# A mixture-of-experts block: choices, ranks, contexts and weight pieces at other tiles, two early pairs, and a shift on ScalarE

## The reference

```python
xij = sigmoid(si[:, :, None] + sj[:, None, :] + b[0])     # si, sj: the context times two vectors
x = x + tanh(g_xattn) * (0.6 * xij + 0.4 * layernorm(x))
y = layernorm(x)                                          # tokens as rows
probs = softmax(y @ wg)                                   # 8 experts
idx, gate = argmax(probs), max(probs)
x = x + tanh(g_ffn) * gate * (y @ W[idx].T + b[idx])
```

## Time and profile before

| | us |
|---|---|
| median of three runs (610.95 to 768.54) | 611.22 |
| the profiled execution | 611.13 |
| its span, from first to last instruction | 609.5 |
| first product of the first expert starts | 177.3 |
| TensorE busy in the span | 521.3 |
| VectorE busy | 405.4 |
| POOL busy | 353.7 |
| ScalarE busy | 292.8 |

### The profile page before, as it was taken

One profiled execution on the slowest core, in us unless ns is written; L12 is line 12 of the kernel. 1 busy time (PEld: TensorE's weight loads), 2 busy tenths in 40 slices (PEclk: granted clock), 3 DMA queues, 4 the chain that ended last, 5 costly groups with the idle time before them and its releaser, 6 DMA issues.

```text
span 609.5 us, 14906 instructions
## 1 busy us (share of the span) xinstructions
PE 521.3 (86%) x2890; PEld 427.8 (70%) x2891; DVE 405.4 (67%) x538; ACT 292.8 (48%) x426; POOL 353.7 (58%) x536
## 2 busy tenths in 40 slices
PE   5577786566689993999999999999999999989980
PEld 5466675455568782888888888788888888878860
DVE  0866567899864675777777577877667757774330
ACT  2584656655522453554554445545354545453330
POOL 3685878875655551655645656556555565565651
PEclk9596778856759996999999999999999999999995
DMA  7942776997766675888888588798759867785520
GB/s 251 389 164 96 247 274 210 326 288 225 256 272 194 186 230 153 243 240 236 266 223 235 177 258 255 215 270 243 213 164 268 228 200 210 240 241 158 188 96 13
DMA packets 87755, 134.67 MB, mean 221 GB/s; under 512 B 11696, under 2 KB 69552, under 8 KB 87728
## 3 DMA queue, kind: packets, MB, share of 16 engines
q1 hardware_dynamic: 71504, 80.28, 46.9%
q0 software_dynamic: 15264, 54.06, 25.0%
q10 hardware_dynamic: 960, 0.00, 0.1%
HBM read 100.49 MB, written 35.91 MB: 224 GB/s over the span
## 4 chain that ended last, share of the span: by engine, by line
PE 34%; DVE 18%; issue 14%; POOL 10%; ACT 10%; ACTq 4%; POOLq 3%; DMA 3%; DVEq 1%; SPq 0%
PE pair L1241 24%; PE pair L1158 4%; DVE pair L929 3%; DVE xr L868 3%; DVE xt L921 3%; DVE raw L857 3%; ACT xt L714 3%; ACT rb L722 2%; POOL scal L559 2%; POOL scal L562 2%; DMA gates<-in_L_xattn_b 2%; PE pair L1149 2%; PE pair L1170 1%; ACT th L680 1%; DVE wt L908 1%
## 5 line engine op out<-in xcount | busy, mean ns | idle before, releaser
L1241 PE MATMUL pair<-wt,xt 128*128 (+1 forms) x1728 | 402.2, 395 | 13.0 <-DVE wt L937 12.9
L1241 PEld LDWEIGHTS pair<-wt,xt 128*128 128x128 f32 x1728 | 327.7, 190 | 87.1 <-issue 14.6
L921 DVE TENSOR_TENSOR xt<-pair,xt 128x1024 f32 (+1 forms) x38 | 46.5, 1225 | 68.3 <-ACT xt L714 68.3
L544 POOL TENSOR_TENSOR rows<-rows,rb 128x1024 f32<-128x1024 f32 x36 | 86.9, 2415 | 3.0 <-ACT rb L736 1.6
L708 ACT ACTIVATE wt<-pair 128x1024 f32 x54 | 55.5, 1028 | 58.0 <-DVE pair L929 54.2
L1158 PE MATMUL pair<-ident,xr 128*128 128x128 f32 x256 | 50.4, 362 | 36.9 <-DVE xr L868 36.9
L736 ACT ACTIVATE rb<-bias_bc,scal 128x1024 f32 (+1 forms) x37 | 46.0, 1244 | 70.6 <-POOL scal L566 70.6
L937 DVE TENSOR_TENSOR wt<-pair,wt 128x1024 f32 (+1 forms) x56 | 67.9, 1212 | 12.5 <-ACT wt L708 12.5
L1158 PEld LDWEIGHTS pair<-ident,xr 128*128 128x128 f32 x256 | 41.8, 192 | 44.1 <-DVE xr L868 36.1
L929 DVE STREAM_TRANSPOSE pair<-w_raw 128x1024 f32<-128x1024 f32 x56 | 69.4, 1240 | 3.5 <-DMA w_raw<-in_L_ffn_W 1.9
L579 POOL DMA_INDIRECT out_x<-rows,scatter_row x36 | 38.8, 1079 | 28.4 <-issue 26.9
(11 more groups left out here) (152 smaller groups left out, 420.0 us busy)
## 6 DMA issues: line engine op xcount, KB each, us to landing
w_raw<-in_L_ffn_W SPq DMA_DIRECT2D x264, 128.0 KB, 3.2
xb<-table SPq DMA_DIRECT2D x156, 128.0 KB
rows<-table POOLq DMA_DIRECT2D x38, 520.0 KB, 5.4
xr<-in_x SPq DMA_DIRECT2D x32, 512.0 KB, 7.3
ctx_in<-in_ctx SPq DMA_DIRECT2D x8, 512.0 KB, 6.1
bias_bc<-in_L_ffn_b SPq DMA_DIRECT2D x8, 512.0 KB, 6.7
out_x<-rows,scatter_row POOLq DMA_INDIRECT x36, 3.8
table<-xr,pos POOLq DMA_INDIRECT x32, 4.3
```

The costliest lines, as they stand in the source:

```text
L544: nc.gpsimd.tensor_tensor(rows[:, k, 0:H], rows[:, k, 0:H], rb[:, :], ALU.add).then_inc(base_ready, 1)
L921: nc.vector.tensor_tensor(xt[:, at, 1, :, :].rearrange("p a k n -> p (a k n)"), ps[:, :], xt[:, at, 0, :, :].rearrange("p a k n -> p (a k ...
L1241: last = nc.tensor.matmul(out_ps[r % 2][:, HALF * h:HALF * (h + 1)], xt[:, r % RING, x_part, k, :], wt[:, bass.ds(par, 1), w_part, k, HALF ...
```

## The change

The choice of a group g < 6 goes one tile later on VectorE, ahead of that tile's statistics; its rank goes ahead of the next tile's turns on TensorE, its position to that tile on VectorE; POOL's stores go one tile later each, and two more of group 6's stay at the last tile. The contexts 4 to 7 go to tiles 4, 7, 10 and 13, with ScalarE's steps one tile later each, ahead of the copy. The weight pieces go to earlier tiles, with the low part at the very next tile; SP's piece loads stand behind other tiles. ScalarE makes `ln_b` in a new function `shift`; POOL negates `ln_ma` once a group for it. Two pairs of the second expert are made before the slot loop.

```diff
-    WEIGHT_TILES = [18, 20, 21, 22, 24, 25, 26, 28]
-    ROW_TILES = [29, 31]
+    WEIGHT_TILES = [17, 18, 20, 21, 22, 24, 25, 26]
+    ROW_TILES = [28, 31]
+    EARLY_PAIRS = 2
+    PIECE_BEHIND = [27, 28, 30, 31]
...
-            return 2 * (g - 2) if g < 4 else GR * (g - 3)
+            return 2 * (g - 2) if g < 4 else 4 + 3 * (g - 4)
+        def chosen_at(g):
+            return GR * (g + 1) + (2 if g < NG - 2 else 1)
...
-                if t == RX + 8:
+                if t == RX + 7:
                     for m in range(WR):
                         load_piece(0, m)
-                if t in (RX + 11, RX + 14, RX + 15):
-                    m = {RX + 11: 3, RX + 14: 4, RX + 15: 5}[t]
+                if t in PIECE_BEHIND:
+                    m = WR + PIECE_BEHIND.index(t)
                     sp.wait_ge(w_turned, m - WR + 1)
                     load_piece(0, m)
...
+            for n in range(2):
+                sp.wait_ge(w_turned, K + n + 1)
+                load_next(K + 2 + n, n)
             for s in range(RX):
                 sp.wait_ge(row_stored[s], 16 * (T // RX))
...
                 link(nc.gpsimd.tensor_tensor(ln_ma[:, four], of_group(g, MEAN), ln_a[:, four], ALU.mult))
+                nc.gpsimd.tensor_scalar(ln_ma[:, four], ln_ma[:, four], -1.0, None, ALU.mult).then_inc(scales_of_tile, 1)
             def linear(t):
                 s = slot_of(t)
-                pool.wait_ge(th_ready, t + 1)
-                link(nc.gpsimd.tensor_scalar(ln_b[:, t:t + 1], xr[:, s, TH:TH + 1], nc2h[:, 0:1], ln_ma[:, t:t + 1],
-                                             ALU.mult, ALU.subtract))
+                pool.wait_ge(shift_ready, t + 1)
...
-                if r == 3 and g > 0:
-                    store(GR * (g - 1))
-                    store(GR * (g - 1) + 1)
-                if r < 2 and g > 1:
-                    store(GR * (g - 2) + 2 + r)
+                if r == 0 and g > 1:
+                    store(GR * (g - 2))
+                    store(GR * (g - 2) + 1)
+                if r in (1, 2) and g > 1:
+                    store(GR * (g - 2) + 1 + r)
...
+            def shift(t):
+                act.wait_ge(th_ready, t + 1)
+                act.wait_ge(scales_of_tile, t // GR + 1)
+                nc.scalar.activation(ln_b[:, t:t + 1], xr[:, slot_of(t), TH:TH + 1], ACT.Identity,
+                                     scale=nc2h[:, 0:1], bias=ln_ma[:, t:t + 1]).then_inc(shift_ready, 1)
...
                 if t + RTH - 1 < T:
                     half_tanh(t + RTH - 1)
+                for n in range(4, NG):
+                    if ctx_turn_tile(n) + 1 == t:
+                        context_copy(n)
+                    if ctx_turn_tile(n) + 2 == t:
+                        context_sums(n)
+                    if ctx_turn_tile(n) + 3 == t:
+                        context_spread(n)
                 if r == 1 and g > 0:
                     logits_copy(g - 1)
+                if t + RTH - 2 < T:
+                    shift(t + RTH - 2)
                 copy_turned(t)
...
-                if r == 2 and g > 0:
+                if g > 0 and chosen_at(g - 1) + 1 == t:
                     position(g - 1)
+                if g > 0 and chosen_at(g - 1) == t and g < NG - 1:
+                    choose(g - 1)
                 if t + LEAD < T:
                     stats(t + LEAD)
                     moments(t + LEAD)
-                if r == 1 and g > 0:
+                if r == 1 and g == NG - 1:
                     choose(g - 1)
...
-            link(nc.vector.tensor_scalar(kinds[:, :], n_begun[:, :], 1.0, None, ALU.is_equal))
+            link(nc.vector.tensor_scalar(kinds[:, :], n_begun[:, :], 1.0, float(EARLY_PAIRS), ALU.is_equal, ALU.mult))
...
+            dve.wait_ge(xt_ready, 2)
+            turn_pair(PAIRS, 0, cut_b)
+            turn_pair(PAIRS, 1, cut_a)
...
+            pair_low(PAIRS, 0, cut_b)
+            pair_low(PAIRS, 1, cut_a)
             finish(0, 0, 0, beyond_early[:, 0:1])
...
+                if g > 0 and chosen_at(g - 1) + 1 == t:
+                    rank(g - 1)
                 turn_tile(t)
...
-                if r == 2 and g > 0:
-                    rank(g - 1)
```

More of the change, by code:

```diff
@@ L225, in build @@
         lin_ready = sem("lin_ready")
+        scales_of_tile = sem("scales_of_tile")
+        shift_ready = sem("shift_ready")
         xc_ready = sem("xc_ready")
@@ L339, in _, with load_piece @@
             sp.dma_start(bias_bc[:, 0, :], bias[0:1, :].to_broadcast([P, H])).then_inc(bias_landed, 16)
+            def load_piece(e, m):
+                for q in (0, 2, 1, 3):
+                    sp.dma_start(w_raw[32 * q:32 * (q + 1), m % WR, :, :],
+                                 in_blocks(W[bass.ds(e, 1), P * m:P * (m + 1), :].rearrange("a o h -> (a o) h"),
+                                           q)).then_inc(w_landed[m % WR], 16)
             for g in range(4, 7):
@@ L344, in _ @@
             next_context(7)
-            def load_piece(e, m):
-                for q in (0, 2, 1, 3):
-                    sp.dma_start(w_raw[32 * q:32 * (q + 1), m % WR, :, :],
-                                 in_blocks(W[bass.ds(e, 1), P * m:P * (m + 1), :].rearrange("a o h -> (a o) h"),
-                                           q)).then_inc(w_landed[m % WR], 16)
             for t in range(RX + 2, T):
                 next_tile(t)
-                if t == RX + 8:
+                if t == RX + 7:
                     for m in range(WR):
                         load_piece(0, m)
-                if t in (RX + 11, RX + 14, RX + 15):
-                    m = {RX + 11: 3, RX + 14: 4, RX + 15: 5}[t]
+                if t in PIECE_BEHIND:
+                    m = WR + PIECE_BEHIND.index(t)
                     sp.wait_ge(w_turned, m - WR + 1)
                     load_piece(0, m)
-            for m in range(6, K):
-                sp.wait_ge(w_turned, m - WR + 1)
-                load_piece(0, m)
+            sp.wait_ge(w_turned, K - WR)
+            load_piece(0, K - 1)
             sp.wait_ge(th_ready, 3 * TB)
@@ L391, in _ @@
             for n in range(2):
-                sp.wait_ge(w_turned, K + n + 1)
-                load_next(K + 2 + n, n)
+                sp.wait_ge(w_turned, K + 2 + n + 1)
+                load_next(K + 4 + n, n)
             sp.wait_ge(xb_turned, 3)
@@ L533, in _ @@
                     linear(t + 2)
-                if r == 3 and g > 0:
-                    store(GR * (g - 1))
-                    store(GR * (g - 1) + 1)
-                if r < 2 and g > 1:
-                    store(GR * (g - 2) + 2 + r)
+                if r == 0 and g > 1:
[3 more added lines that the diff above has]
+                    store(GR * (g - 2) + 1 + r)
+                if t == T - 1:
+                    store(T - 2 * GR)
+                    store(T - 2 * GR + 1)
             for t in range(T - GR - 2, T):
@@ L748, in _ @@
                 context_spread(g)
+            act.wait_ge(scales_ready, 1)
             for t in range(RTH - 1):
                 half_tanh(t)
+                if t:
+                    shift(t - 1)
             for t in range(T):
@@ L763, in _ @@
                     xt_high(1, 1, cut_a)
-                for n in range(2, NG):
+                for n in range(2, 4):
                     if ctx_turn_tile(n) == t:
@@ L771, in _ @@
             logits_copy(NG - 1)
[L773 to L777, removed]
+            square(0, 0)
+            exp_sum(0, 0)
+            scaled_bias(0, 0, 0, 0)
             for n in range(RX):
@@ L781, in _ @@
                 cut_high(1, n, 1, ps)
+            square(1, 1)
+            exp_sum(1, 1)
+            scaled_bias(1, 1, 0, 0)
+            xt_high(2, 2, cut_a)
+            for n, ps in enumerate((cut_b, cut_a)):
+                cut_high(1, 2 + n, 1, ps)
             settled(summed, 2)
@@ L970, in _ @@
                 add_tanh(t)
+                if t - 1 in WEIGHT_TILES:
+                    cut_low(0, WEIGHT_TILES.index(t - 1), 0, cut_a)
                 if t in WEIGHT_TILES:
[L972 to L979, removed]
+                    dve.wait_ge(si_ready, NG)
+                    dve.wait_ge(sj_ready, NG)
+                    turn_weights(0, WEIGHT_TILES.index(t), cut_a)
+                if t == EARLY_TILES + GR + 1:
                     count_early()
                 if t == ROW_TILES[0]:
-                    cut_low(0, K - 1, 0, cut_a)
                     dve.wait_ge(w_ready, K)
@@ L1226, in _ @@
                         sum_context(n)
+                    if ctx_turn_tile(n) + (1 if n < 4 else 2) == t:
                         spread_context(n)
```

14 lines of the change are left out of this document (7 added, 7 removed).

## The result

Over 19 runs the changed kernel's median is 613.3 us against 610.1 for the kernel before; the ratio is 1.0051, with a 95% interval from 1.0031 to 1.0071. It is a little slower, and the forecast was 600.7. On that chip the medians were 617.8 and 610.38, ratio 1.0114 (1.0082 to 1.0146). The two intervals don't meet, and no run shows why the same kernel came out 4.5 us apart. The experiments are compared with 617.8, which like most of them is a median of four executions; measured from 613.3, what each of them brings back to the changed kernel is 4.5 less.

A forecast was written before the change was run, and what follows sets the result against it. VectorE was taken as the first stage's spine, with TensorE waiting for weights in the passage and full behind 240 us. From 611.13, minus 2.4 (first stage) and 8.0 (passage), came 600.7 us; range 590 to 614.

The forecast's parts named there:

- A7: End of VectorE's add of tile 7 in the first stage: forecast 54.3 us, 57.65 before.
- The logits and ranks together: VectorE's waits for logits by token and for ranks, first stage: together under 8 us; before, 16.9 and 9.2.
- Statistics wait for loads: First stage: new waits of VectorE's statistics on tile loads, 2 to 6 us in each of three groups.
- the row turn for its blocks: At tile 28, VectorE's row turn waits for the block loads, which need tile 19's store: 5.6 us.
- The chain behind A31: From tile 31's add (forecast 166.1) through turn, route, logits, choice, rank, totals to the first product (174.9): unchanged.
- passage: Passage to the second expert: second early pair shrinks TensorE's weight gap from 10.66 to 2.7; gain 8.0, between 5 and 10.7.
- three rounds of 17.8: Tiles 8 to 19, four per round: turn, copy, tanh, shift, scaling, store, load, statistics, add, 17.8 us each; 53.4 in all.
- A15: End of VectorE's add of tile 15 in the first stage: forecast 89.9 us, 95.34 before.
- A19: End of VectorE's add of tile 19 in the first stage: forecast 107.7 us, 6.5 earlier than before.
- A11: End of VectorE's add of tile 11 in the first stage: forecast 72.1 us, 76.23 before.
- The shift itself: ScalarE's shift per tile in the first stage, moved from POOL: taken as 0.25 us, between 0.17 and 0.4.
- Rival (b): Tiles 8 to 19: slower store and load landings make each round 24.6 us; total 621.1, slower than before; chance 0.12.

## Why the prediction was wrong

**Held.** A7 came at 54.75 for 54.3, with the mechanism named. The logits and ranks together wait 5.7, under the 8 forecast. Statistics wait for loads (11.1 in all, most of it in the first two rounds) and the row turn for its blocks (4.7, forecast 5.6). The chain behind A31 is unchanged: 186.91 - 178.2 = 8.7, before 8.8.

**The account**, by medians: passage 6.2, contexts 6.4 and pieces 2.3 won, 22.3 lost by late choices and ScalarE's shift, in all 7.4 slower (617.8 - 610.4). For the contexts the forecast had counted nothing.

**The step that failed: three rounds of 17.8.** They were 20.6, 18.0 and 23.8 (A15 is 93.3), 62.4 for 53.4, so A19 came 9.4 late and the first product 12.0 late. In the first round, 2.8 too long, the terms were: to the end of tile 10's scaling 8.0, where 6.5 and its handovers were summed (with the turn at 2.0, which took 1.1), store 5.4 for 4.1, load 4.3 for 4.0, statistics and add as summed. So the queues took 1.2 too much (2.1 with the turn as it was), the landings 1.6. The chain was the right one, its path through the queues and its landings mis-sized. The sum took each handover on ScalarE and POOL as a matter of 0.05, for which no row stood, that is, it followed one tile through the engines and let the queues stand empty. They weren't: ScalarE stood in front of an earlier shift, waiting for POOL, whose negation took 1.18 where 0.2 off the path was put down; and POOL's store stood behind a scaling, waiting for ScalarE. "ScalarE's order now decides when POOL may scale" stands in the prediction, as the reason to count no gain; that it is a loss was not priced. With the shift back on POOL, choices still late, the first round took 14.5 (A7 52.37, A11 66.82); the second and third took 20.6 and 21.1, with waits for loads and a weight piece.

The shift itself was a mis-sized term too: 0.39, not 0.25, at the top of its bounds. The row that it was taken from, a 128x4 activation of 0.17, has no scale or shift by column. The Trainium skill, "ScalarE: Activation LUTs", section "What ACT_TABLE_LOAD costs", gives 186 ns for a small activation and some 93 more for each operand that is a column; two of them make an estimated 0.37, and the trace agrees with 0.39. But this 0.14 a tile isn't the loss: the idle activations cost 1.1 in all.

The third round, 6.0 too long, holds 5.28 in front of piece 0, for which the forecast had no term. The piece's loads stand in SP's queue behind tile 23's, and so behind tile 7's store (issued at 92.38, landed 7.1 later, the pieces at 99.88): the same chain again. In the run with early pieces that wait turned into one for tile loads, and nothing was won.

**Rival (b)** named the right place and, with 0.12, was thought unlikely: the slot chain turns against the change. Its price by landings is only part of it. In the changed kernel, the stores issued from 60 to 80 us and then the loads from 64 to 80:

```profile
DMA to landing us min/median/max: 5.4/5.8/7.6
...
DMA to landing us min/median/max: 4.3/6.0/6.8
```

That is 11.8 together, at the 11.6 from which (b) was to decide. But the kernel with old choices and POOL's shift has 5.4 and 4.0 there, and 6.6 and 5.4 from 100 to 120, nearly the 7.1 and 5.0 of the changed kernel, and waits for no load at all. So landings of that size, at least from 100 to 120, don't decide by themselves; they count where the store goes out with no slack left. (b)'s 24.6 came in none of the three rounds.

**The passage: 8.0 forecast, 6.2 alone, 3.2 in the changed kernel's trace.** The gap closed to 3.47, near the 2.7 worked out. Not counted: TensorE's wait for the row tile of slot 2 (1.75 to 2.33), put down at nothing with a bound of 3. Of the 5.4 won in the gaps (10.66 - 1.75 - 3.47) another 1.1 went into the 216 products ahead, 52.7 us where it was 51.6: in the first 15 us the granted clock was 0.81 and 54 matmuls ran, in the kernel before 0.89 and 59. Both are mixtures of the levels 1.2 and 2.4 GHz. In the 20 us ahead TensorE had been busy 12.90 us at a clock of 0.59, in the kernel before 13.47 us at 0.66. With the passage alone the 216 products took 52.9 as well, but there the first 15 us ran at 0.90, and the slow part came behind the 2.33 wait: 37 matmuls in 10 us at 0.83, where the changed kernel had 44 at 1.00 behind its 1.75. The last 1.1 was not followed.

**What stays open.** With the stores first ScalarE's shift still costs 4.5 with old choices (599.83 - 595.36, in overlapping intervals) and 7.2 with late ones (603.73 - 596.56). With late choices the first product shows it, 173.41 against 166.66; with old ones it starts at 166.61 against 165.54, so only 1.1 lies in the first stage. POOL still waits for the shift there (32.0 and 27.3 us), but no run takes this rest apart. Nor is it known why the changed kernel's medians differ, 613.3 and 617.8.

## What to carry to other kernels

Before moving a small operation off a busy engine, ask who waits for its result and what is queued behind the waiter: a 0.4 us shift on another engine, with its inputs from the first and its result wanted there, made two in-order queues stop for each other and cost 10 us over 32 tiles (with old choices), while 32 of the same operation without that tie cost about 1. Where buffers are freed by a store, put the store ahead of anything in its queue that waits for another engine. Removing a wait is no gain where the next one takes its place, as with the logits here. And when each of several single edits brings back nearly the whole loss, combine them: here the store order was worth 0.1 by itself and 14.1 in the kernel whose stores were late.

## What was not expected of the hardware

A 128x4 multiplication by a constant on POOL took 1.18 us beside a VectorE add and 0.24 at another time (53.67 and 71.22 us), the same pattern as the shift in the earlier trace rows; here it stood on the path of a whole group. And from 60 to 80 us the changed kernel's loads and stores took longer to land than those of the kernel before (medians 6.0 for 4.0 and 5.8 for 4.1), though the DMA share was lower there (0.59 for 0.76); no run shows why.
